# Attention operands in four buffers, loaded three pairs ahead, and the scatter DMAs of a pair issued one to each key block

## The chip, the cores and the metric

The kernel runs on 1 core of a Trainium2 chip. The metric is the time of one execution on the device in microseconds. The kernel before took 2875.18 us (median of 3 runs, 2851.36 to 2876.99).

## What is computed

A transformer layer on x of shape (8, 1024, 256), all in float32: x + attention(layernorm(x)) + mixture(layernorm(x)).

```
xn = layernorm(x)
# attention: 16 heads of 16 columns, bias alibi[h, q, k] = slope[h] * (k - q)
Q, K, V = xn @ Wq + bq, xn @ Wk + bk, xn @ Wv + bv
attn = softmax(Q K^T * 0.25 + alibi);  a = (attn V) @ Wo + bo
# mixture: each of the 8192 tokens goes to the 2 best of 8 experts, plus a shared expert
w = softmax(top2(xn @ Wg))
y = sum_e w[e] * (silu(xn W1[e]) * (xn W2[e])) W3[e]  +  (silu(xn Ws1) * (xn Ws2)) Ws3
out = x + a + y
```

## The kernel before

The work runs in four parts, one after the other. **Projections**: the 8192 tokens in 16 groups of 512; normalised rows go to `Xn` in DRAM, Q and K as a high and a low part to `QKh` and `QKl`, V to `Vd`. **Attention**: 64 pairs, a pair being two heads of one batch (8 batches of 8 pairs). **Experts**: 71 blocks of 256 token slots. **Shared expert and output**: 16 groups of 512 tokens.

One class, `Order`, writes down the order of all steps (`run`, L78, and `attention`, L206). Each engine runs through the same order in a subclass of its own (`Tensor`, `Scalar`, `Vector`, `Pool`, `Sync`) and issues its own share, so each engine's instructions, and each DMA queue's, stand in a fixed order. Engines wait for each other by counting semaphores; a wait blocks everything behind it on that engine.

A pair r has eight key blocks kc; a step s is 8r + kc, and `attention` works on even steps for two blocks at once. In the order `ORDER` (L42) TensorE alternates score matmuls ("S", 54 rows by 512 columns, into banks 0 to 3), maximum matmuls ("u", `max_unit`, 52 rows by 512, into a ring of banks 5 to 7) and, after four of each, the value matmuls of an earlier block ("P", `values`). ScalarE takes the exponential of the scores (L771). VectorE reduces each maximum matmul to row maxima (L916). The maxima must be known before a pair's scores are made; so the 32 maximum matmuls of a pair run ahead (`AHEAD`, 48 units, is one pair and a half): those of pair r+2 begin at step 8r + 4, those of pair r+1 end at step 8r + 2. Then VectorE makes 16 numbers of them (L920), GpSimd negates and splits them (L1178 to L1183), TensorE transposes them in the second half of step 8r + 4 (`max_rows`), ScalarE copies them (L760), and SP writes them into rows 52 and 53 of the pair's Q operand (L1354).

The operands of a pair are Q and K as stacked rows (high part, low part, high part, two rows of ones or of maxima, two of the bias) of 1024 columns, in the tile `OPS`, buffer r % 3. SP loads them in `load_pair` (L1328): 16 DMAs, 12 of 64 KB (L1344) and 4 of 8 KB from `Alid` (L1348, the last). `next_pair(r)` (L242) calls it at kc = 0 for pair r+2; between its second and third call stands `heads(r-1, 0)`, for which SP waits for pair r-1's sums (L778). Pairs 0 and 1 are loaded during the projections, pair 2 just before the loop. The rows of ones come from two memsets by GpSimd during the projections (L1135).

`heads` also normalises a finished pair: SP moves its sums out and back as a broadcast (`asum`, L1373, at kc = 4), GpSimd multiplies (L1190, at kc = 6), SP stores the result (L1377).

Beside attention runs the routing of tokens to experts: VectorE has one small operation every fourth step, GpSimd clears the 71 blocks of slots `Xs` and copies the expert weights together (pairs 0 to 9), and in pairs 34 to 49 (`SCAT_AT` = 34) GpSimd writes the normalised rows into their slots: per pair, after kc = 3, one load of 512 rows (L1218) and eight indirect DMAs of 128 rows (L1224), four row blocks by two chosen experts. Buffers `xr` alternate.

Of the kernel before, what the change touches and what calls it, by code (L numbers as in the profile page):

```python
# [7 lines left out]
F32 = mybir.dt.float32  # L8
# [6 lines left out]
P = 128  # L15
NB, S, D = 8, 1024, 256
# [5 lines left out]
NG = N // GT  # L22
# [5 lines left out]
NPAIR = NB * NH // 2  # L28
# [16 lines left out]
SCAT_AT = 34  # L45

SEMS = (

    "c_ident c_bor c_w1 c_w c_ali c_r x0 x1 x2 x3 xn0 xn1 xn2 qh0 qh1 ql0 ql1 vs0 vs1 op0 op1 op2 mx0 mx1 "
    "vst asd sdw asb ox0 ox1 zero wd xg0 xg1 sc0 sc1 wb0 wb1 wb2 xs0 xs1 xs2 xs3 yr0 yr1 xr0 xr1 oro ga0 ga1 ga2 ga3 res "  # L50

    "xt qkmm vmm mxmm mrt smm pv rtmm sct gmm up down sdn "
# [21 lines left out]
class Order:  # L74
# [3 lines left out]
    def run(self):  # L78
# [15 lines left out]
        n = 0  # L94
# [36 lines left out]
        while n < AHEAD:  # L131
            self.max_unit(n)
            n += 1
        for i in range(4):
            self.load_pair(2, i)
        for s in range(8 * NPAIR - 8):
            n = self.attention(s, n)
        for b in range(3):
# [2 lines left out]
        for s in range(8 * NPAIR - 8, 8 * NPAIR):  # L141
            n = self.attention(s, n)
# [3 lines left out]
        for s in range(8 * NPAIR, 8 * NPAIR + 2):  # L146
            n = self.attention(s, n)
# [58 lines left out]
    def attention(self, s, n):  # L206

        r, kc = divmod(s, 8)
        if s % 2 == 0:
            i = v = 0  # L210
            for c in ORDER:
                if c == "S":
                    if r < NPAIR:
                        self.scores(r, kc + i // 4, i % 2, i // 2 % 2)
                    i += 1
                elif c == "u":
                    if n < 32 * NPAIR:
                        self.max_unit(n)
                        n += 1
                else:  # L220
                    if v == 1 and kc == 4 and r + 1 < NPAIR:
                        self.max_rows(r + 1)
                    if s >= 2:
                        self.values(*divmod(s - 2 + v, 8))
                    v += 1
            if kc == 0:
                self.next_pair(r)
            elif r >= 1:
                self.heads(r - 1, kc // 2)
        if r < NE + 2 and kc == 1:  # L230
            self.pack_expert(r)
        if s < NBLK:
            self.clear_slots(s)
        if kc == 3 and SCAT_AT <= r < SCAT_AT + NG:
            self.scatter_group(r - SCAT_AT)
        if kc == 5 and r % 8 in (2, 3) and r < NPAIR - 8:
            self.load_v(r // 8 + 1, r % 8 - 2)
        if s % 4 == 3:
            self.route(s // 4)
        return n  # L240

    def next_pair(self, r):  # L242
        for i in range(4):
            if i == 2 and r >= 1:
                self.heads(r - 1, 0)
            if 1 <= r and r + 2 < NPAIR:
                self.load_pair(r + 2, i)


    def begin(self): pass  # L250
# [17 lines left out]
    def heads(self, r, i): pass  # L268
    def pack_expert(self, e): pass
    def clear_slots(self, s): pass  # L270
    def scatter_group(self, g): pass
    def route(self, i): pass
    def gather_weights(self, b): pass
    def load_slots(self, b): pass
# [42 lines left out]
def build(nc, t, out):  # L317
    ctx = ExitStack()
    with ctx:
        sem = {n: ctx.enter_context(nc.semaphore("s_" + n)) for n in SEMS}  # L320
# [15 lines left out]
        Xs = dram("Xs", [NSLOT, D])  # L336
# [6 lines left out]
        xn_v = Xn.rearrange("(g j p) d -> g p j d", p=P, j=4)  # L343
# [12 lines left out]
        slot = sbuf(ctx, "slot", [P, 2, NT], I32)  # L356
# [5 lines left out]
        mT = sbuf(ctx, "mT", [32, 2, P], F32R)  # L362
        xr = sbuf(ctx, "xr", [P, 2, 4, D])
        OPS = sbuf(ctx, "OPS", [P, 12 * S], F32R)
        QO = OPS[:, 0:3 * S].rearrange("p (k n) -> p k n", k=3)
        KO = OPS[:, 3 * S:6 * S].rearrange("p (k n) -> p k n", k=3)
        VB = sbuf(ctx, "VB", [P, 8 * S])
        vb = VB[:, :].rearrange("p (b c n) -> p b c n", b=2, c=8)

# [99 lines left out]
        class Tensor(Order):  # L469
# [71 lines left out]
            def max_unit(self, n, bank=None):  # L541
                r, u = divmod(n, 32)
                hh, i, half = 1 - u % 2, u // 4, u // 2 % 2
                k, h0 = r % 3, 64 * hh
                self.w.wait_ge(f"op{k}", 256 * (r // 3 + 1))
                if bank is None:
                    bank = self.ring_bank("max", n)
                else:
                    self.w.wait_ge("mxred", n)
                    if n >= 32:  # L550
                        self.w.wait_ge("mrev", 1)
                self.mm(ps[:, bank, :], QO[h0:h0 + KMAX, k, i * P:(i + 1) * P],
                        KO[h0:h0 + KMAX, k, half * GT:(half + 1) * GT], True, True).then_inc(sem["mxmm"], 1)

# [9 lines left out]
                          mneg[:, r % 2, :, :, :].rearrange("p h l i -> p (h l i)")).then_inc(sem["mrt"], 1)  # L564

            def scores(self, r, kc, hh, half):
                k, h0, n = r % 3, 64 * hh, 16 * r + 2 * kc + half
                bank = 2 * (n % 2) + hh
                self.w.wait_ge(f"op{k}", 256 * (r // 3 + 1))
                self.w.wait_ge(f"mx{r % 2}", 32 * (r // 2 + 1))  # L570
                if n < 2:
                    self.w.wait_ge("xh", NG)
                    self.w.wait_ge("xl", NG)
                self.w.wait_ge("exp", n - 1)
                if kc == 6 and half == 0:
                    self.w.wait_ge("mrev", min(r + 2, NPAIR))
                q = self.mm(ps[:, bank, :], KO[h0:h0 + KEXP, k, kc * P:(kc + 1) * P],
                            QO[h0:h0 + KEXP, k, half * GT:(half + 1) * GT], True, True)
                if hh == 1:
                    q.then_inc(sem["smm"], 1)  # L580
# [531 lines left out]
        class Pool(Order):  # L1112
# [15 lines left out]
            def pad(self, i):  # L1128
                e = self.e
                if i < 4:  # L1130
                    self.w.wait_ge("rstd", i + 2)
                    self.w.wait_ge("vad", i - 1)
                    self.w.wait_ge("pad", i)
                if i < 2:
                    e.memset(OPS[64 * i + 32:64 * i + 64, 0:6 * S].bitcast(F32), 1.0).then_inc(sem["pad"], 1)  # L1135
                elif i == 2:
                    e.memset(VB[:, :], 0.0).then_inc(sem["pad"], 1)
                elif i == 3:
                    e.memset(vb.rearrange("p b c (h d) -> p (b c) h d", d=32)[:, :, :, HD:HD + 1], 1.0
                             ).then_inc(sem["pad"], 1)  # L1140
# [71 lines left out]
                                 zero[:, :].rearrange("p (u d) -> p u d", u=1).broadcast_to([P, 2, D])  # L1212
                                 ).then_inc(sem["zero"], 16)

            def scatter_group(self, g):
                e, k = self.e, g % 2
                self.w.wait_ge(f"sc{k}", 128 * (g // 2))
                e.dma_start(xr[:, k, :, :], xn_v[g]).then_inc(sem[f"xg{k}"], 16)  # L1218
                self.w.wait_ge("rts", 2)
                self.w.wait_ge("zero", 16 * NBLK)  # L1220
                self.w.wait_ge(f"xg{k}", 16 * (g // 2 + 1))
                for i in range(4):
                    for c in range(2):
                        e.indirect_dma_start(  # L1224
                            Xs[:, :], bass.IndirectOffsetOnAxis(ap=slot[:, c, 4 * g + i:4 * g + i + 1], axis=0),
                            xr[:, k, i, :], None).then_inc(sem[f"sc{k}"], 16)

            def gather_weights(self, b):
                k = b % 3
# [52 lines left out]
        class Sync(Order):  # L1282
# [44 lines left out]

            def load_pair(self, r, i):  # L1328
                b, j = divmod(r, NH // 2)
                k = r % 3  # L1330
                at = slice(b * S, (b + 1) * S)
                done = sem[f"op{k}"]
                self.w.wait_ge("pad", 2)
                self.w.wait_ge("c_ali", 16)
                self.w.wait_ge("smm", 16 * (r - 2))
                self.w.wait_ge("mxmm", 32 * (r - 2))
                for f in range(2):
                    self.w.wait_ge(f"qh{f}", 16 * (b + 1))
                    self.w.wait_ge(f"ql{f}", 16 * (b + 1))
                dst, o, parts, al = ((QO, 0, (QKh, QKl, QKh), 1), (KO, D, (QKh, QKh, QKl), 0))[i // 2]  # L1340
                for n in (0, 1) if i % 2 == 0 else (2,):
                    for h in range(2):
                        h0 = o + 32 * j + HD * h
                        self.e.dma_start(dst[64 * h + 16 * n:64 * h + 16 * n + 16, k, :].bitcast(F32),  # L1344
                                         parts[n][h0:h0 + HD, at]).then_inc(done, 16)
                if i % 2:
                    for h in range(2):
                        self.e.dma_start(dst[64 * h + 48 + 2 * al:64 * h + 50 + 2 * al, k, :].bitcast(F32),  # L1348
                                         Alid[al, 2 * j + h, :, :]).then_inc(done, 16)

            def max_rows(self, r, bank=None):
                self.w.wait_ge("mrev", r + 1)
                for hh in range(2):
                    self.e.dma_start(QO[64 * hh + 52:64 * hh + 54, r % 3, :].bitcast(F32).rearrange("l (i n) -> l i n", n=P),  # L1354
                                     mT[16 * hh:16 * hh + 16, r % 2, :].bitcast(F32)).then_inc(sem[f"mx{r % 2}"], 16)

            def heads(self, r, i):
# [118 lines left out]
```

## Time and profile before

| | |
|---|---|
| median of 3 runs | 2875.18 us |
| the profiled execution, its own time | 2872.02 us |
| its span | 2870.2 us |
| mean granted TensorE clock | 0.943 |
| TensorE busy | 2639.1 us (92%) |
| VectorE busy | 2119.3 us (74%) |
| ScalarE busy | 1644.3 us (57%) |
| GpSimd busy | 854.4 us (30%) |
| chain that ended last: TensorE matmuls (L474) | 57% |
| the same: VectorE maxima (L916) | 8% |
| the same: SP issuing operand loads (L1344) | 6% |
| the same: landing of the last operand load (`OPS<-Alid`) | 3% |

Busy time is the sum over one engine's instructions. In the rows further down PE is TensorE, PEld its weight loads, DVE VectorE, ACT ScalarE, POOL GpSimd and SPq the DMA-issuing queue of SP. The granted clock is a share of full speed; it has two levels, 1.2 and 2.4 GHz, so that 0.5 is the low one. `OPS<-Alid` names a DMA by what it writes and reads. The chain is followed back from the last instruction through whatever released each step.

### The profile page before, as it was taken

How to read it: one execution, taken by the hardware profiler on the slowest of the kernel's cores; microseconds unless marked ns; L12 is line 12 of the kernel's file. 1: busy time of each engine (PE TensorE's matmuls, PEld its weight loads, DVE VectorE, ACT ScalarE, POOL GpSimd, SP SyncE). 2: the span in 40 equal slices, each digit the busy share in tenths (PEclk: the TensorE clock that was granted, in tenths of full speed). 3: DMA queues.
4: the chain of work that ended last, by engine and by line, in shares of the span. 5: the costliest groups of instructions: out<-in, count | busy, mean ns of one | idle time of the engine just before them, and what ended most of it. 6: DMA issues, size and time to landing. Idle time of an engine off the chain costs nothing.

```text
span 2870.2 us, 42979 instructions
## 1 busy us (share of the span) xinstructions
PE 2639.1 (92%) x16090; PEld 1624.0 (57%) x16090; DVE 2119.3 (74%) x3518; ACT 1644.3 (57%) x2314; POOL 854.4 (30%) x920
## 2 busy tenths in 40 slices
PE   5999889999999998888888999999999999999998
PEld 4774333333333333333333333399999998788887
DVE  7878777888988876766777888567777775545544
ACT  2445555666677665555655667767777773322322
POOL 4334433101101003434332100133343434434433
PEclk8998888999999987877888999999999999999999
DMA  5985553222222213333333211267777773433432
GB/s 194 349 297 181 175 176 123 73 59 69 70 62 76 61 53 104 107 100 111 106 102 95 66 58 58 97 213 233 244 237 242 241 232 88 122 89 95 120 95 74
DMA packets 213359, 383.62 MB, mean 134 GB/s; under 512 B 45264, under 2 KB 134544, under 8 KB 203792
## 3 DMA queue, kind: packets, MB, share of 16 engines
q1 hardware_dynamic: 175040, 218.25, 24.3%
q0 software_dynamic: 37024, 161.83, 17.8%
q8 instruction: 128, 2.10, 0.3%
q10 hardware_dynamic: 1088, 0.79, 0.1%
q14 instruction: 79, 0.65, 0.1%
HBM read 248.84 MB, written 141.43 MB: 136 GB/s over the span
## 4 chain that ended last, share of the span: by engine, by line
PE 59%; DVE 15%; SPq 8%; issue 6%; DMA 5%; ACT 5%; another core or an unknown queue 1%; POOL 1%; ACTq 0%; DVEq 0%; POOLq 0%
PE ps L474 57%; DVE mx L916 8%; SPq L1344 6%; DMA OPS<-Alid 3%; DVE OPS L1087 3%; PE ps L487 2%; ACT pta L771 2%; DVE VB L1084 2%; SPq L1365 1%; ACT OPS L843 1%; ACT accs L778 1%; DMA asum<-Sd 1%; SPq L1348 1%; DVE OL L1073 1%
## 5 line engine op out<-in xcount | busy, mean ns | idle before, releaser
L916 DVE TENSOR_REDUCE mx<-ps 128x1 f32<-128x512 f32 x2048 | 1277.0, 684 | 318.6 <-PE ps L474 277.5
L474 PE MATMUL ps<-OPS 52*128 52x512 f32 (+1 forms) x4096 | 964.7, 470 | 137.3 <-DMA OPS<-Alid 48.5
L474 PEld LDWEIGHTS ps<-OPS 52*128 52x128 f32 (+1 forms) x4096 | 501.7, 202 | 902.0 <-DVE mx L916 280.1
L771 ACT ACTIVATE pta<-ps 128x1024 f32<-128x1024 f32 x512 | 497.7, 1022 | 361.0 <-PE ps L474 329.0
L771 ACT ACTIVATE ptb<-ps 128x1024 f32<-128x1024 f32 x512 | 497.0, 1023 | 217.0 <-PE ps L474 207.6
L474 PE MATMUL ps<-OPS,WB 128*128 128x256 f32 (+1 forms) x2268 | 363.6, 312 | 4.2 <-DVE VB L1055 2.8
L474 PEld LDWEIGHTS ps<-OPS,WB 128*128 128x128 f32 x2268 | 310.5, 180 | 33.6 <-issue 4.8
L474 PE MATMUL ps<-ptb,VB 128*32 128x512 f32 x2048 | 310.3, 682 | 0.0
L474 PE MATMUL ps<-pta,VB 128*32 128x512 f32 x2048 | 287.9, 636 | 0.0
L474 PE MATMUL ps<-OPS,WB0c 128*128 128x256 f32 (+3 forms) x1440 | 257.9, 330 | 4.0 <-DVE WB0c L1038 3.0
L474 PEld LDWEIGHTS ps<-OPS,WB0c 128*128 128x128 f32 (+1 forms) x1440 | 210.3, 181 | 34.3 <-issue 5.1
L1190 POOL TENSOR_TENSOR accs<-accs,asum 128x512 f32<-128x512 f32 x64 | 82.4, 1288 | 488.8 <-DMA asum<-Sd 488.6
L474 PE MATMUL ps<-WB,OPS 128*128 128x256 f32 (+1 forms) x1422 | 189.7, 284 | 27.1 <-DVE OPS L1087 27.1
L1178 POOL TENSOR_SCALAR m<-m 128x16 f32<-128x16 f32 x64 | 19.5, 305 | 608.8 <-DVE m L920 608.8
L474 PEld LDWEIGHTS ps<-WB,OPS 128*128 128x128 f32 (+1 forms) x1422 | 178.7, 191 | 33.7 <-issue 33.6
L1060 DVE TENSOR_TENSOR OPS<-VB,OPS 128x256 fp32r<-128x256 f32 (+1 forms) x213 | 151.4, 711 | 37.2 <-ACT OPS L813 37.2
L837 ACT ACTIVATE VB<-ps 128x512 f32<-128x512 f32 (+1 forms) x96 | 57.1, 594 | 196.9 <-PE ps L474 196.9
L1087 DVE TENSOR_TENSOR OPS<-VB,OPS 128x512 fp32r<-128x512 f32 (+1 forms) x96 | 111.8, 1165 | 66.1 <-ACT OPS L843 39.3
L1224 POOL DMA_INDIRECT Xs<-xr,slot x128 | 124.7, 974 | 96.4 <-DMA xr<-Xn 62.2
L1098 DVE SCALAR_TENSOR_TENSOR VB<-gath,prob,ps 128x256 f32<-128x256 f32 x64 | 26.5, 477 | 162.3 <-PE ps L474 162.3
L843 ACT CAST OPS<-VB 128x512 fp32r<-128x512 f32 (+1 forms) x96 | 59.8, 623 | 145.4 <-DVE VB L1084 119.4
L1266 POOL DMA_INDIRECT gath<-Ys,slot x128 | 128.3, 1002 | 36.5 <-issue 35.2
(154 smaller groups left out, 2871.6 us busy)
## 6 DMA issues: line engine op xcount, KB each, us to landing
OPS<-QKh SPq DMA_DIRECT2D x512, 64.0 KB
Xs<-zero POOLq DMA_DIRECT2D x71, 256.0 KB, 3.6
xr<-Xs SPq DMA_DIRECT2D x71, 256.0 KB
Ys<-VB SPq DMA_DIRECT2D x71, 256.0 KB
QKh<-qkH SPq DMA_DIRECT2D x16, 1024.0 KB, 6.1
QKl<-qkL SPq DMA_DIRECT2D x16, 1024.0 KB, 8.4
OPS<-QKl SPq DMA_DIRECT2D x256, 64.0 KB
asum<-Sd SPq DMA_DIRECT2D x64, 256.0 KB
```

Source lines behind the costliest of these rows:

```text
L474: return self.e.matmul(o, l, r, start=start, stop=stop)
L487: return self.e.transpose(o, in_, ident[:, :])
L771: self.e.activation(pt(n), ps[:, b:b + 2, :], ACT.Exp).then_inc(sem["exp"], 1)
L843: self.e.copy(HH[0:hn, s, :], hf[0:hn, k, :]).then_inc(sem["hh"], 1)
L916: e.reduce_max(mx[:, k2, hh, i, half:half + 1], ps[:, bank, :], AX.X).then_inc(sem["mxred"], 1)
L1060: e.tensor_tensor(HL[0:hn, s, 0:BT], hfq[0:hn, k, :], HH[0:hn, s, 0:BT].bitcast(F32), ALU.subtract).then_inc(sem["hl"], 1)
L1084: e.tensor_tensor(hf[0:hn, k, :], ps[0:hn, 3 + 2 * (n % 2), :], sg[0:hn, k, :], ALU.mult).then_inc(sem["hf"], 1)
L1087: e.tensor_tensor(HL[0:hn, s, :], hf[0:hn, k, :], HH[0:hn, s, :].bitcast(F32), ALU.subtract).then_inc(sem["hl"], 1)
L1190: self.e.tensor_tensor(accs[:, r % 2, :], accs[:, r % 2, :], asum[:, :], ALU.mult).then_inc(sem["nrm"], 1)
L1224: e.indirect_dma_start(Xs[:, :], bass.IndirectOffsetOnAxis(ap=slot[:, c, 4 * g + i:4 * g + i + 1], axis=0), xr[:, k, i, :], None).then_inc ...
L1266: self.e.indirect_dma_start(gath[:, j, c, :], None, Ys[:, :], bass.IndirectOffsetOnAxis(ap=slot[:, c, i:i + 1], axis=0)).then_inc(sem[f"ga ...
L1344: self.e.dma_start(dst[64 * h + 16 * n:64 * h + 16 * n + 16, k, :].bitcast(F32), parts[n][h0:h0 + HD, at]).then_inc(done, 16)
```

## The change

The operands get four buffers in place of three: `QO` and `KO` take 4096 columns each of `OPS`, which had that room (12288 columns in all), the memsets cover 8192 columns, every `r % 3` becomes `r % 4`, and there is a semaphore `op3`. `load_pair` waits for the scores and maxima of three pairs back, is called three pairs ahead in `next_pair`, and pair 3 is loaded with pair 2 before the loop.

`scatter_group`, called once at kc = 3 of a pair, becomes `scatter_rows`, called at every kc. The first call of a pair also loads the rows; each call issues one of the eight indirect DMAs, after a wait for the scores of all blocks before its own (`smm` at least 16r + 2kc).

```diff
@@ Order.run
-        for i in range(4):
-            self.load_pair(2, i)
+        for r in (2, 3):
+            for i in range(4):
+                self.load_pair(r, i)
@@ Order.attention
-        if kc == 3 and SCAT_AT <= r < SCAT_AT + NG:
-            self.scatter_group(r - SCAT_AT)
+        if SCAT_AT <= r < SCAT_AT + NG:
+            self.scatter_rows(r - SCAT_AT, kc, 16 * r + 2 * kc)
@@ Order.next_pair
-            if 1 <= r and r + 2 < NPAIR:
-                self.load_pair(r + 2, i)
+            if 1 <= r and r + 3 < NPAIR:
+                self.load_pair(r + 3, i)
@@ build
-        QO = OPS[:, 0:3 * S].rearrange("p (k n) -> p k n", k=3)
-        KO = OPS[:, 3 * S:6 * S].rearrange("p (k n) -> p k n", k=3)
+        QO = OPS[:, 0:4 * S].rearrange("p (k n) -> p k n", k=4)
+        KO = OPS[:, 4 * S:8 * S].rearrange("p (k n) -> p k n", k=4)
@@ Tensor.max_unit and Tensor.scores
-                self.w.wait_ge(f"op{k}", 256 * (r // 3 + 1))
+                self.w.wait_ge(f"op{k}", 256 * (r // 4 + 1))
@@ Pool.pad
-                    e.memset(OPS[64 * i + 32:64 * i + 64, 0:6 * S].bitcast(F32), 1.0).then_inc(sem["pad"], 1)
+                    e.memset(OPS[64 * i + 32:64 * i + 64, 0:8 * S].bitcast(F32), 1.0).then_inc(sem["pad"], 1)
@@ Pool
-            def scatter_group(self, g):
+            def scatter_rows(self, g, i, n):
+
                 e, k = self.e, g % 2
-                self.w.wait_ge(f"sc{k}", 128 * (g // 2))
-                e.dma_start(xr[:, k, :, :], xn_v[g]).then_inc(sem[f"xg{k}"], 16)
+                if i == 0:
+                    self.w.wait_ge(f"sc{k}", 128 * (g // 2))
+                    e.dma_start(xr[:, k, :, :], xn_v[g]).then_inc(sem[f"xg{k}"], 16)
                 self.w.wait_ge("rts", 2)
                 self.w.wait_ge("zero", 16 * NBLK)
                 self.w.wait_ge(f"xg{k}", 16 * (g // 2 + 1))
-                for i in range(4):
-                    for c in range(2):
-                        e.indirect_dma_start(
-                            Xs[:, :], bass.IndirectOffsetOnAxis(ap=slot[:, c, 4 * g + i:4 * g + i + 1], axis=0),
-                            xr[:, k, i, :], None).then_inc(sem[f"sc{k}"], 16)
+                self.w.wait_ge("smm", n)
+                j, c = divmod(i, 2)
+                e.indirect_dma_start(
+                    Xs[:, :], bass.IndirectOffsetOnAxis(ap=slot[:, c, 4 * g + j:4 * g + j + 1], axis=0),
+                    xr[:, k, j, :], None).then_inc(sem[f"sc{k}"], 16)
@@ Sync.load_pair
-                k = r % 3
+                k = r % 4
...
-                self.w.wait_ge("smm", 16 * (r - 2))
-                self.w.wait_ge("mxmm", 32 * (r - 2))
+                self.w.wait_ge("smm", 16 * (r - 3))
+                self.w.wait_ge("mxmm", 32 * (r - 3))
```

## Rows read from the trace of the kernel before

**Rows 1.** Busy time by stretch of attention; columns end with clock, DMA share, GB/s.
```profile
259.00:580.00 321.00, 289.38 (x1558) 114.46 (x1556) 256.49 (x437) 195.13 (x218) 101.80 (x157) 0.88 0.43 136
580.00:1077.00 497.00, 465.89 (x2713) 182.54 (x2714) 431.18 (x738) 340.93 (x379) 50.03 (x92) 0.98 0.22 63
1077.00:1574.00 497.00, 433.04 (x2199) 169.61 (x2196) 346.39 (x579) 277.91 (x307) 180.75 (x222) 0.82 0.34 104
1574.00:1827.00 253.00, 238.45 (x1417) 93.20 (x1413) 221.81 (x374) 177.72 (x198) 23.36 (x46) 1.00 0.21 62
```

**Rows 2.** Timeline (start us, us): the copies ending pairs 0, 12, 33, 50, 61.
```profile
259.24 0.59 ACT L778 COPY accs<-ps 128x512 f32<-128x512 f32 x1
...
580.03 0.59 ACT L778 COPY accs<-ps 128x512 f32<-128x512 f32 x1
...
1076.83 0.59 ACT L778 COPY accs<-ps 128x512 f32<-128x512 f32 x1
...
1573.52 0.59 ACT L778 COPY accs<-ps 128x512 f32<-128x512 f32 x1
...
1827.40 0.59 ACT L778 COPY accs<-ps 128x512 f32<-128x512 f32 x1
```

**Rows 3.** Waits (us in total, times, longest) in the four stretches, in order.
```profile
PE ps L474 <- DMA OPS<-Alid: 18.2, 11, 3.6
...
PE ps L474 <- DMA OPS<-Alid: 10.0, 21, 1.5
...
PE ps L474 <- DMA OPS<-Alid: 15.7, 9, 6.0
...
PE ps L474 <- DMA OPS<-Alid: 4.5, 11, 0.6
```

**Rows 4.** Timeline of a calm pair's middle, around the last operand load.
```profile
1666.12 2.48 DVE L916 TENSOR_REDUCE mx<-ps 128x1 f32<-128x512 f32 x4 [0.22 <-PE ps L474]
...
1668.84 2.48 DVE L916 TENSOR_REDUCE mx<-ps 128x1 f32<-128x512 f32 x4 [0.23 <-PE ps L474]
...
1669.86 0.57 SPq L1348 DMA_DIRECT2D OPS<-Alid  x2
...
1672.07 1.77 PE L474 MATMUL ps<-OPS 52*128 52x512 f32 x7 [0.57 <-DMA OPS<-Alid]
...
1672.60 2.49 DVE L916 TENSOR_REDUCE mx<-ps 128x1 f32<-128x512 f32 x4 [0.90 <-PE ps L474]
```

**Rows 5.** Timeline of VectorE after a long load wait in the first stretch.
```profile
404.93 2.48 DVE L916 TENSOR_REDUCE mx<-ps 128x1 f32<-128x512 f32 x4 [2.25 <-PE ps L474]
409.10 2.48 DVE L916 TENSOR_REDUCE mx<-ps 128x1 f32<-128x512 f32 x4 [1.69 <-PE ps L474]
```

**Rows 6.** Timeline of one burst of scatters: first, eighth, and VectorE beside it.
```profile
1417.71 1.03 POOL L1224 DMA_INDIRECT Xs<-xr,slot  x1 [3.85 <-DMA xr<-Xn]
...
1421.86 2.49 DVE L916 TENSOR_REDUCE mx<-ps 128x1 f32<-128x512 f32 x4 [0.23 <-issue]
...
1426.65 0.96 POOL L1224 DMA_INDIRECT Xs<-xr,slot  x1 [0.30 <-issue]
...
1427.67 1.29 DVE L916 TENSOR_REDUCE mx<-ps 128x1 f32<-128x512 f32 x2 [3.33 <-remote]
```

**Rows 7.** Waits in the third stretch with no releaser on record.
```profile
DVE mx L916 <- remote: 25.4, 9, 4.3
```

**Rows 8.** GpSimd: a normalisation and a negation (timeline); the row load's landing.
```profile
1660.80 1.28 POOL L1190 TENSOR_TENSOR accs<-accs,asum 128x512 f32<-128x512 f32 x1 [11.25 <-DMA asum<-Sd]
...
1671.63 0.25 POOL L1178 TENSOR_SCALAR m<-m 128x16 f32<-128x16 f32 x1 [9.55 <-DVE m L920]
...
DMA to landing us min/median/max: 4.2/4.4/5.3
```

**Rows 9.** Timeline: the second memset and the VectorE operation beside it.
```profile
28.15 5.70 DVE L890 TENSOR_SCALAR xn<-xt,mv,rstd 128x256 f32<-128x256 f32 x2 [0.54 <-POOL rstd L1126]
28.17 5.21 POOL L1135 MEMSET OPS<- 32x6144 f32 x1
```

More of the change, by code:

```diff
@@ L47 @@
 SEMS = (
-    "c_ident c_bor c_w1 c_w c_ali c_r x0 x1 x2 x3 xn0 xn1 xn2 qh0 qh1 ql0 ql1 vs0 vs1 op0 op1 op2 mx0 mx1 "
+    "c_ident c_bor c_w1 c_w c_ali c_r x0 x1 x2 x3 xn0 xn1 xn2 qh0 qh1 ql0 ql1 vs0 vs1 op0 op1 op2 op3 mx0 mx1 "
     "vst asd sdw asb ox0 ox1 zero wd xg0 xg1 sc0 sc1 wb0 wb1 wb2 xs0 xs1 xs2 xs3 yr0 yr1 xr0 xr1 oro ga0 ga1 ga2 ga3 res "
@@ L270, in clear_slots, with scatter_rows @@
     def clear_slots(self, s): pass
-    def scatter_group(self, g): pass
+    def scatter_rows(self, g, i, n): pass
     def route(self, i): pass
@@ L543, in max_unit @@
                 hh, i, half = 1 - u % 2, u // 4, u // 2 % 2
-                k, h0 = r % 3, 64 * hh
-                self.w.wait_ge(f"op{k}", 256 * (r // 3 + 1))
+                k, h0 = r % 4, 64 * hh
+                self.w.wait_ge(f"op{k}", 256 * (r // 4 + 1))
                 if bank is None:
@@ L566, in scores @@
             def scores(self, r, kc, hh, half):
-                k, h0, n = r % 3, 64 * hh, 16 * r + 2 * kc + half
+                k, h0, n = r % 4, 64 * hh, 16 * r + 2 * kc + half
                 bank = 2 * (n % 2) + hh
-                self.w.wait_ge(f"op{k}", 256 * (r // 3 + 1))
+                self.w.wait_ge(f"op{k}", 256 * (r // 4 + 1))
                 self.w.wait_ge(f"mx{r % 2}", 32 * (r // 2 + 1))
@@ L1353, in max_rows @@
                 for hh in range(2):
-                    self.e.dma_start(QO[64 * hh + 52:64 * hh + 54, r % 3, :].bitcast(F32).rearrange("l (i n) -> l i n", n=P),
+                    self.e.dma_start(QO[64 * hh + 52:64 * hh + 54, r % 4, :].bitcast(F32).rearrange("l (i n) -> l i n", n=P),
                                      mT[16 * hh:16 * hh + 16, r % 2, :].bitcast(F32)).then_inc(sem[f"mx{r % 2}"], 16)
```

## The prediction

> **What bounds the kernel now.** I read the views in this order: the stages, the pair boundaries, the waits on the operand loads, one calm pair at close range, then the same pair where the clock is low and where the scatters run.
>
> The stage table [rows 1] shows TensorE busy for 90% and more of every attention stage, but at a granted clock of 0.88, 0.98, 0.82 and 1.00. The evictions at pair ends [rows 2] cut the same stretches into pairs: 12 pairs in 320.8 us (26.7 each), 21 in 496.8 (23.7), 17 in 496.7 (29.2), 11 in 253.9 (23.1). One pair is the same work throughout, so the late stage is the kernel undisturbed, and the first and third stages carry an excess: 3.6 us by 12 pairs and 6.1 us by 17.
>
> TensorE waits for the last operand load (the Alid rows) once in nearly every pair: 18.2, 10.0, 15.7 and 4.5 us by stage [rows 3]. In a calm pair [rows 4] four maxima start at 1666.12 and at 1668.84, a step of 2.72 us, and the next four at 1672.60, a step of 3.76: the Alid load was issued at 1669.86 and TensorE got it at 1672.07, 0.57 us late.
>
> A longer wait costs more than itself. After one that left VectorE idle for 2.25 us the steps go from 404.93 to 409.10 [rows 5], which is 4.17 us for the work of 2.72. A microsecond at the low clock (1.2 of 2.4 GHz) thus wastes 1 - 2.72/4.17 = 0.35 us. By the mean clock, 2 x (1 - 0.88) = 24% of the first stage, 77 us, and 2 x (1 - 0.82) = 36% of the third, 179 us, ran low [rows 1].
>
> The third stage is the one with the scatters. A burst of eight runs from 1417.71 to 1427.61 [rows 6]; VectorE ends its maxima at 1424.35 and gets the next only at 1427.67, when the last scatter has been issued. The records name no releaser; nine such holds sum to 25.4 us on VectorE [rows 7]. The first five scatters of that burst go by without a hold.
>
> **The change, part by part.** *Loads three pairs ahead.* The same sixteen DMAs of a pair are issued by SP at the same place and behind the same counts of finished score and maximum matmuls, since both the buffer count and the distance grow by one. They are needed a whole pair, some 23 us, later than now; the largest wait to be hidden is 6 us. Every such wait goes except that of pair 2, loaded just before the loop as now. Pair 3 is now loaded there too: sixteen more issues, about 8 us of SP (two Alid issues take 0.57 us [rows 4], the others are similar), while SP's next duty is half a pair away. In exchange the loop's last load falls away.
> What is late next in the calm boundary step is VectorE itself: it has two small operations there. The gain is between the wait alone, 4.5/11 = 0.4 us a pair, and the whole 1.04 us of the longer step; I take 0.6, nearer to the wait as VectorE is nearly full, so a pair is worth 22.5.
> - Late stage: 11 x 0.6 = 7 us.
> - Second stage: from 23.7 to 22.75 a pair (22.5 and a quarter for the routing operations that run there) gives 19 us; the bounds are its waits, 10, and 25 at 22.5.
> - First stage: from 26.7 to 23.2 (more routing, and a heavier DMA load) gives 42 us. From the other side: waits of 18.2 and 0.35 x 77 = 27 for the clock are 45.
>
> *Scatters spread.* The third stage at 22.6 a pair instead of 29.2 would give 112 us. From the other side: 0.35 x 179 = 62 for the clock, 15.7 for load waits, 25.4 or more of holds: 103 and up. Of this the loads own 15.7, their 0.6 a pair where no wait shows, and the low clock behind them; I put that at 33, and 79 to the bursts.
> They will not be one to each block. GpSimd's queue is in order, and three things stand in it: the normalisation, which starts at 1660.80 [rows 8], just ahead of a pair's end; the scatters of blocks 6 and 7 behind it, 2 x 1.27 us [rows 6]; then the load of the next rows, about 1 to issue, as for a scatter, and 4.4 to land, with GpSimd waiting for it [rows 8]. That is 1662.1 + 2.5 + 5.4 = 1670.0. Scatters 0 and 1 then end at 1672.5, the negation of the maxima, due at 1671.63, starts 0.9 us late, and scatters 2 to 5 follow at once, as the score blocks they wait for are done or nearly: a run of six with a gap of some 0.8, the negation's, then a run of two. Behind the negation TensorE's transpose is two steps (5.4 us) away, so its 0.9 us cost nothing; if that cover is gone, see the third rival. The waits on score counts release themselves and hold nothing that is due. Six in a run is near where the hold began (after 6.6 us), so I keep back 20 us. The term is 92; ends 33 and 112.
> On this the Trainium skill, SBUF — State Buffer, section "SBUF: two separate sides", speaks against the change: engine ports and DMA ports are disjoint and neither side can slow the other. By that rule the holds are none of the scatters' doing, and the term would be 33, not 92. The rows put the hold's end on the burst's end, so I go by them.
>
> *Padding for the fourth buffer.* Two memsets on GpSimd grow from 6144 to 8192 columns. One takes 5.21 us [rows 9], so 6.95, +1.74 each. A VectorE operation that starts with it lasts 5.70 us, to the memset's end, and TensorE waits out that stretch: nothing hides it, +3.5 us (from 0, were it not on the path).
> The Trainium skill, same page and section, calls the pair of ports shared by GpSimd and VectorE an exclusive lock; the 5.70 us agree.
>
> *Rest.* The new wait names no other engine's queue; buffers and later stages reuse the same memory after attention ends. Nothing changes from 1865 us on.
>
> **Sum.** 42 + 19 + 92 + 7 - 3.5 = 156 us off the profiled execution's own 2872.0: 2716 us. The median of the runs shown is 3 us above it, and they spread from 2851 to 2877.
>
> **The rivals.**
> 1. *The holds stay*, moved into the run of six. For: no row names what holds the engines; the run of six. Against: five scatters pass free, and the end of the hold is the end of the burst. Term 33 in place of 92: 2872 - (42 + 19 + 33 + 7 - 3.5) = 2775.
> 2. *Depth helps, another load-like wait follows it* (the maxima rows of the next pair, or the broadcast of the sums, late in the first stage's traffic). The first stage then gives half, and the clock stays low there: 2716 + 21 = 2737, inside the forecast's range.
> 3. *GpSimd's queue becomes the bound in the scatter pairs.* If the normalisation comes over 4.5 us later than in the calm pair (5.4 less 0.9), the transpose waits, and each of 16 pairs pays some 2 us and 8 us at the low clock, 5 in all: +80, 2796; with rival 1, 2855, which is no change.
> 4. *Slower: every scatter holds the engines by itself.* Place: each of the 16 scatter pairs, eight times. If one hold of about 0.8 us per block keeps the clock low, a pair costs 8 x (4.17 - 2.72) = 11.7 and 8 x 0.8 = 6.4 more than 22.5; 16 x 18.1 = 290 against the 112 of excess now, less the 64.5 of the other terms: +113, 2985. It decides from any hold that keeps the clock low throughout. Against it: the free first five.
>
> **How the numbers follow.** The forecast with rival 2 has 0.62, rival 1 0.23, rival 3 0.10 (half of it with rival 1), rival 4 0.05. The forecast's own range is 2680 (every term at its better end) to 2755. To hold 8 in 10 the range goes on through rival 1 and the milder rival 3: 2680 to 2800. A measurement of this kernel tells about 1%, 29 us. Faster by more has 0.88, within it 0.07 (rival 3 with 1, and part of what no case names), slower 0.05.
>
> **What would show each step.** Right: no wait on the Alid load after pair 2; clock near 1.0 in the first stage; pairs of 22.4 to 22.8 in the late stage; scatter pairs near 23 to 24 with no hold of over 1 us on VectorE; the memsets at 6.95. Scatters in runs of six and two would confirm the queue's reading. Wrong: holds at the end of each run of six (rival 1), TensorE's transpose waiting for GpSimd (3), a clock near 0.5 through the third stage (4), or boundary steps still above 3.3 us with the loads long landed.

## The result and the profile after

The changed kernel took 2719.6 us (median of 4 runs, 2717.9 to 2722.7) beside 2865.4 us of the kernel before (4 runs, 2851.4 to 2877.0): a ratio of 0.949, 95% interval 0.944 to 0.955. Its profiled execution has a span of 2717.9 us against 2870.2 and a mean granted clock of 0.982 against 0.943. Timed again in another placing (a placing is a chip and the time at which it was used), beside the kernel before there, it took 2720.8 us against 2835.5: 0.960 (0.955 to 0.964). The change is worth 4 to 5%. The changed kernel ran alike in both placings and the kernel before did not, which matters below. The three later placings were on three chips; the record doesn't name the chip of the first, so it is open whether the chip made the difference.

The copies that end pairs 0, 12, 33, 50 and 61 of the changed kernel, as in [rows 2] (timeline: start, duration):

```profile
262.88 0.59 ACT L779 COPY accs<-ps 128x512 f32<-128x512 f32 x1
...
560.50 0.59 ACT L779 COPY accs<-ps 128x512 f32<-128x512 f32 x1
...
1033.49 0.59 ACT L779 COPY accs<-ps 128x512 f32<-128x512 f32 x1
...
1430.57 0.59 ACT L779 COPY accs<-ps 128x512 f32<-128x512 f32 x1
...
1674.58 0.59 ACT L779 COPY accs<-ps 128x512 f32<-128x512 f32 x1
```

The stages between them, in the view of [rows 1] (busy time of TensorE, its weight loads, VectorE, ScalarE and GpSimd, then clock, DMA share, GB/s):

```profile
263.00:561.00 298.00, 269.41 (x1558) 106.20 (x1557) 254.57 (x438) 195.20 (x218) 101.33 (x157) 0.95 0.46 147
561.00:1033.00 472.00, 445.81 (x2707) 174.70 (x2703) 428.27 (x737) 339.62 (x378) 49.93 (x93) 1.00 0.24 66
1033.00:1431.00 398.00, 370.63 (x2203) 145.87 (x2200) 342.40 (x581) 276.40 (x308) 181.23 (x221) 0.97 0.44 130
1431.00:1675.00 244.00, 233.96 (x1423) 91.88 (x1420) 220.59 (x375) 178.31 (x199) 23.28 (x46) 1.00 0.21 60
```

VectorE is busy with the same reductions for as long as before, but in shorter stretches, and the clock is 0.95 to 1.00 where it was 0.82 to 1.00. By the copies the stages went from 320.8, 496.8, 496.7 and 253.9 us to 297.6, 473.0, 397.1 and 244.0. That is 23.2 + 23.8 + 99.6 + 9.9 = 156.5 us; the first pair ends 3.6 us later, and what lies behind pair 61 takes 0.5 more: 152.3, the difference of the spans.

The boundary step of a calm pair, as in [rows 4]:

```profile
1500.16 2.48 DVE L917 TENSOR_REDUCE mx<-ps 128x1 f32<-128x512 f32 x4 [0.22 <-PE ps L475]
1502.68 0.19 DVE L921 TENSOR_REDUCE m<-mx 128x16 f32<-128x32 f32 x1
1502.78 0.24 DVE L926 RECIPROCAL sq<-sq 128x16 f32<-128x16 f32 x1
1502.94 2.42 DVE L917 TENSOR_REDUCE mx<-ps 128x1 f32<-128x512 f32 x4
1505.59 2.48 DVE L917 TENSOR_REDUCE mx<-ps 128x1 f32<-128x512 f32 x4 [0.24 <-PE ps L475]
```

The step from 1500.16 to 1502.94 takes 2.78 us instead of 3.76, and the next 2.65: TensorE no longer waits for a load there, and VectorE's two small operations are absorbed. A calm pair takes 22.18 us against 23.08.

A pair that is still long, in the scatter stage of the changed kernel (pair 35, 25.4 us; the lines show its first half):

```profile
1058.85 0.59 SPq L1368 DMA_DIRECT2D sq<-accs  x1
...
1063.35 0.25 DVE L926 RECIPROCAL sq<-sq 128x16 f32<-128x16 f32 x1 [1.91 <-DMA sq<-accs]
...
1063.99 0.99 POOL L1227 DMA_INDIRECT Xs<-xr,slot  x1 [5.69 <-DMA xr<-Xn]
1064.20 0.50 PE L475 MATMUL ps<-OPS 52*128 52x512 f32 x1 [2.08 <-DVE mx L917]
...
1065.29 0.97 POOL L1227 DMA_INDIRECT Xs<-xr,slot  x1 [0.30 <-issue]
1066.30 0.29 POOL L1179 TENSOR_SCALAR m<-m 128x16 f32<-128x16 f32 x1
...
1067.43 1.06 POOL L1227 DMA_INDIRECT Xs<-xr,slot  x1 [0.20 <-issue]
```

Two things are to be seen. VectorE, whose instructions are in order, stands at the reciprocal of the finished pair's sums until SP's fetch of those sums (`sq<-accs`) lands, 4.5 us after its issue; TensorE then waits for VectorE, 2.1 us. This is the wait that took the load's place. The issue itself is late as well: SP issued the fetch 3.2 us after the start of the copy that ends the pair (1055.67), where 0.6 us is the usual figure. And GpSimd issues scatters 0 and 1 when the row load has landed, then the negation of the maxima, then scatters 2 to 5: the order that the prediction worked out. With scatters 6 and 7 behind the normalisation, they go out in runs of two, two and four.

The memsets (source line; min/median/max in ns, then first and last start) and the VectorE operation beside the second, as in [rows 9]:

```profile
L1136 POOL MEMSET OPS<- x2: 6919/6920/6921, 19.2 to 29.7; 32x8192 f32 x2
```
```profile
29.67 7.41 DVE L891 TENSOR_SCALAR xn<-xt,mv,rstd 128x256 f32<-128x256 f32 x2 [0.54 <-POOL rstd L1127]
```

### The profile page after: what moved, and what is told of

Same layout as the page of the kernel before. It is cut to its first block, busy times and chain, and to the rows that moved or that the text cites. A ratio compares the mean times of both kernels' runs of the same rounds, so it can differ in the third digit from the quotient of the medians.

```text
span 2717.9 us, 42994 instructions
## 1 busy us (share of the span) xinstructions
PE 2527.5 (93%) x16090; PEld 1580.8 (58%) x16090; DVE 2114.4 (78%) x3518; ACT 1639.8 (60%) x2314; POOL 858.1 (32%) x920
## 4 chain that ended last, share of the span: by engine, by line
PE 62%; DVE 22%; issue 6%; ACT 5%; DMA 4%; SPq 1%; POOL 1%; ACTq 0%; DVEq 0%; POOLq 0%
PE ps L475 60%; DVE mx L917 13%; DVE OPS L1088 3%; ACT pta L772 2%; PE ps L488 2%; DVE VB L1085 2%; DMA sq<-accs 2%; ACT OPS L844 1%; SPq L1347 1%; DVE OL L1074 1%; ACT OPS L826 1%; DMA WR0c<-Wd,widx 1%; DVE VB L1105 0%; DVE xn L891 0%; DMA xt<-in_x 0%
## 5 line engine op out<-in xcount | busy, mean ns | idle before, releaser
L917 DVE TENSOR_REDUCE mx<-ps 128x1 f32<-128x512 f32 x2048 | 1270.6, 681 | 160.2 <-PE ps L475 152.3
L475 PE MATMUL ps<-OPS 54*128 54x512 f32 (+1 forms) x4096 | 897.0, 443 | 89.3 <-DVE mx L917 41.3
L475 PEld LDWEIGHTS ps<-OPS 52*128 52x128 f32 (+1 forms) x4096 | 461.6, 189 | 797.2 <-DVE mx L917 279.3
L475 PE MATMUL ps<-ptb,VB 128*32 128x512 f32 x2048 | 279.7, 619 | 0.0
L475 PE MATMUL ps<-pta,VB 128*32 128x512 f32 x2048 | 276.2, 612 | 0.0
L1061 DVE TENSOR_TENSOR OPS<-VB,OPS 128x256 fp32r<-128x256 f32 (+1 forms) x213 | 152.3, 715 | 35.8 <-ACT OPS L814 35.8
```

Source lines behind the costliest of these rows:

```text
L475: return self.e.matmul(o, l, r, start=start, stop=stop)
L917: e.reduce_max(mx[:, k2, hh, i, half:half + 1], ps[:, bank, :], AX.X).then_inc(sem["mxred"], 1)
L1061: e.tensor_tensor(HL[0:hn, s, 0:BT], hfq[0:hn, k, :], HH[0:hn, s, 0:BT].bitcast(F32), ALU.subtract).then_inc(sem["hl"], 1)
```

## The experiments

The theory at the start was the prediction's: load waits and scatter bursts each cost by themselves (A). The rival (B): what shows at a burst comes from meeting the loads. All stage times are differences of the copies' starts in one profiled execution each; the two kernels without holds, before again and memsets only, differ by 12 us in the third stage, so a few microseconds there mean little. The kernel before took 2836.1 us beside the spread-only, four-buffers, memset and plain-DMA kernels, 2835.5 beside the second runs and both sums-first kernels, and 2838.1 beside the last two.

| kernel | median us | ratio to before, 95% | stage 1 | stage 2 | stage 3 | stage 4 |
|---|---|---|---|---|---|---|
| before, first profile | 2865.4 | | 320.8 | 496.8 | 496.7 | 253.9 |
| before again | 2835.2 (one run) | | 319.0 | 500.1 | 458.9 | 253.8 |
| memsets only | 2839.3 (one run) | | 314.4 | 494.1 | 470.7 | 255.3 |
| spread only | 2817.7 | 0.992 (0.990-0.995) | 318.4 | 490.3 | 446.7 | 253.8 |
| four buffers only | 2738.3 | 0.964 (0.960-0.968) | 294.8 | 473.1 | 422.2 | 244.1 |
| changed, first profile | 2719.6 | 0.949 (0.944-0.955) | 297.6 | 473.0 | 397.1 | 244.0 |
| changed again | 2720.8 | 0.960 (0.955-0.964) | 296.4 | 473.0 | 401.7 | 244.1 |
| four buffers, plain DMAs in a burst | 2709.1 (one run) | | 297.6 | 473.1 | 387.0 | 244.0 |
| sums first, burst | 2702.2 | 0.952 (0.949-0.956) | 283.0 | 472.8 | 392.5 | 244.1 |
| sums first | 2695.3 | 0.950 (0.946-0.954) | 281.9 | 473.0 | 386.0 | 244.0 |
| rows ahead | 2687.0 | 0.945 (0.942-0.949) | 288.2 | 473.0 | 377.2 | 244.1 |
| late pad | 2689.0 | 0.945 (0.942-0.949) | 287.6 | 473.1 | 377.3 | 244.1 |

**Four buffers only.** The changed kernel with its burst back:

```diff
-        if SCAT_AT <= r < SCAT_AT + NG:
-            self.scatter_rows(r - SCAT_AT, kc, 16 * r + 2 * kc)
+        if kc == 3 and SCAT_AT <= r < SCAT_AT + NG:
+            for i in range(8):
+                self.scatter_rows(r - SCAT_AT, i, 0)
```

> The changed kernel with the eight scatters again in one burst after kc = 3 (four buffers and three pairs ahead stay). Theory A (the holds belong to the burst, whatever the loads do): stages 1, 2 and 4 as in the changed kernel (297.6, 473.0, 244.0 us), the 17 pairs of the third stage keep holds of 2 to 4 us at the burst's end and a low clock behind them, 397 + about 79 = 460 to 480 us; total about 2795 us, 0.975 of before. Rival B (the holds came from the burst meeting operand loads that were wanted at once): third stage 390 to 410 us, total about 2725 us.

It is neither. The third stage is 422.2 us, below A's 460 and above B's 410, and no wait without a releaser is on record in it. VectorE's waits in that stage (us, times, longest) are for the fetch of the sums:

```profile
DVE sq L927 <- DMA sq<-accs: 23.6, 12, 8.8
```

Why the fetch is late here stands in the timeline of one such pair, from the burst's last scatter on:

```profile
1110.92 0.96 POOL L1228 DMA_INDIRECT Xs<-xr,slot  x1 [0.30 <-issue]
1111.90 1.29 POOL L1192 TENSOR_TENSOR accs<-accs,asum 128x512 f32<-128x512 f32 x1
1112.84 0.59 ACT L780 COPY accs<-ps 128x512 f32<-128x512 f32 x1
1113.22 0.34 SPq L1381 DMA_DIRECT2D OTd<-accs  x1
1113.79 0.79 SPq L1348 DMA_DIRECT2D OPS<-QKh  x2
...
1117.99 0.60 SPq L1369 DMA_DIRECT2D sq<-accs  x1
...
1119.91 0.25 DVE L927 RECIPROCAL sq<-sq 128x16 f32<-128x16 f32 x1 [1.31 <-DMA sq<-accs]
```

GpSimd's normalisation of the pair before stands behind the burst; SP's queue stands at the store of the normalised rows (`OTd<-accs`) until it is done, and the eight loads and then the fetch come behind that store. From issue to reciprocal the fetch takes only 1.9 us. Eleven of the twelve waits are of this kind: 1.9 to 2.6 us from issue to reciprocal, but an issue 4.3 to 6.1 us after the copy's start. The twelfth is issued 10.0 us after it. With four buffers a burst costs through this chain, from GpSimd's queue to SP's to VectorE's, and not by holding the engines.

**Spread only.** The kernel before with `scatter_rows` and its call in place of `scatter_group`.

> The kernel before (three buffers, two pairs ahead) with the scatters spread as in the changed kernel. Theory A: no hold without releaser in the third stage, but load waits stay; stages 1, 2 and 4 as before (320.8, 496.8, 253.9 us), third stage 497 - 79 = about 418 to 435 us; total about 2790 to 2805 us, 0.975 of before. Rival B: third stage still 480 us and more, total within 1% of before. If the two parts add, the gains of this run and of the four-buffers-only run sum to 152 us; if one needs the other they sum to less.

The gain is 0.8% (0.5 to 1.0), not 2.5%. With that of four buffers alone it sums to the whole: 98 + 18 = 116 us, where the changed kernel gained 115 when it was timed again. So the parts add, within what the runs can tell, and theory A's sizes are wrong. TensorE's load waits in the third stage remain, all of them:

```profile
PE ps L474 <- DMA OPS<-Alid: 26.8, 17, 2.7
```

**Memsets only.**

```diff
-  e.memset(OPS[64 * i + 32:64 * i + 64, 0:6 * S].bitcast(F32), 1.0)
+  e.memset(OPS[64 * i + 32:64 * i + 64, 0:8 * S].bitcast(F32), 1.0)
```

> The kernel before with the two memsets widened from 6144 to 8192 columns and nothing else. Memsets of 6.95 us each; the first pair's sums are copied at about 262.8 us in place of 259.24 (both memsets on the path, +3.5); if only one were on it, about 261.0; if none, 259.2. Nothing else moves.

The memsets take 6.92 us. The first copy is at 263.4 us, 4.2 later than in the first profile and 1.9 later than in the second profile of the kernel before (261.5). That starting time varies from execution to execution by more than one memset's share, so this run alone leaves the size between 1.9 and 4.2. All profiles together say more: the three with both early memsets short have the copy at 259.2, 261.5 and 259.7 us, the eight with them wide at 262.9 to 265.6, with means of 260.1 and 263.8. That is 3.6 us, near the forecast 3.5, though seven of the eight differ in more than the memsets. The surprise was elsewhere: the same bursts, and none of the holds of [rows 6, 7].

**Before again.** The kernel before, unchanged.

> The kernel before, word for word, profiled beside the next kernels. If the holds without a releaser in the third stage belong to the kernel, they are there again, 25 us and more, in ten bursts or more, and the third stage takes about 497 us. If they belonged to the one execution or chip that was profiled first (the memset run, with the same bursts, had none and took 471 us there), none is there and the third stage takes 465 to 475 us.

No hold. Its third stage takes 458.9 us, and its waits there are for loads, more of them than in [rows 3]:

```profile
PE ps L474 <- DMA OPS<-Alid: 42.4, 17, 9.4
DVE sq L925 <- DMA sq<-accs: 15.2, 2, 7.8
```

So the holds do not come with the code alone. They were there in the first profile, in a placing where the kernel before took 2851 to 2877 us, and absent in all ten profiles of the three later placings; four of these have the same scatter bursts. A hold of TensorE would also give a late load time to land, which would explain why 15.7 us of load waits were seen with holds and 42.4 without (53.3 in memsets only); no run shows this by itself.

**Plain DMAs in a burst.** Four buffers only, with each scatter replaced by a plain DMA of the same 128 KB to fixed rows, so that the rows do not reach their experts' slots and the kernel's result is wrong:

```diff
-  e.indirect_dma_start(Xs[:, :], bass.IndirectOffsetOnAxis(ap=slot[...], axis=0), xr[:, k, j, :], None)
+  e.dma_start(Xs[(8 * g + i) * P:(8 * g + i + 1) * P, :], xr[:, k, j, :])
```

> As the four-buffers-only kernel, but each of the eight indirect DMAs of the burst is a plain DMA of the same 128 KB from the same rows to fixed, contiguous rows of the slots (so the rows do not reach their experts' slots), still issued by GpSimd. If the holds come from the generation of descriptors for scattered rows by GpSimd: no hold, third stage near 380 to 400 us. If they come from eight 128 KB writes in a row from GpSimd's queue, whatever the form: holds as with the scatters, third stage 460 us and more.

387.0 us, 35 below the burst of scatters, and no hold. As the burst of scatters had no hold beside it either, this can't tell what made them. What it does show: the sums' fetch is waited for 4.9 us in this stage, against 23.6 with the scatters. GpSimd is through with eight plain DMAs in 4.3 us and with eight scatters in 9.9 (1101.94 to 1111.88), so the normalisation, and SP's queue behind it, are held up less:

```profile
1097.60 4.30 POOL L1228 DMA_DIRECT2D Xs<-xr  x8 [3.67 <-DMA xr<-Xn]
```

**Changed again.** The changed kernel, unchanged.

> The changed kernel, word for word, timed beside the kernel before on one chip: the size of the change where the kernel before ran at 2836 us. If the first comparison's two sides were equally placed: ratio 0.949, about 2692 us there. If the kernel before alone varies from chip to chip and the changed one does not: about 2719 us, ratio 0.959.

0.960 and 2720.8 us: the kernel before is what varied. Between the two profiles of this placing the stages gain 22.6 + 27.1 + 57.2 + 9.8 us, 116.0 with the start and the tail.

**Sums first.** One reordering in the changed kernel:

```diff
     def next_pair(self, r):
+        if r >= 1:
+            self.heads(r - 1, 0)
         for i in range(4):
-            if i == 2 and r >= 1:
-                self.heads(r - 1, 0)
             if 1 <= r and r + 3 < NPAIR:
                 self.load_pair(r + 3, i)
```

> The changed kernel with one reordering in next_pair: SP fetches the finished pair's sums before all four operand loads, not between the second and the third. Theory: what is late next in the first and third stages is VectorE's reciprocal, which waits for that fetch (13 waits, 43.9 us with one of 25 at the end of attention), standing in the DMA queues behind the loads of Q. With the fetch ahead of 8 of the 64 KB loads it lands earlier: the pairs of 25 to 30 us go down to 22.2 to 24, first stage 285 us, third stage 380 to 385 us, total about 2690 us. Rival (the fetch is slow because of the software queue's traffic, not of the loads): same waits, 2719 us.

2695.3 us, 25 less than the changed kernel beside it (runs of 2691.9 to 2699.2 against 2717.6 to 2728.0). Besides the wait at the end of attention, the fetch is waited for once, 1.1 us. The first stage gets 14.4 us shorter and the third 15.6 (in these two profiles the part behind pair 61 is 7.5 longer, so the spans differ by 21.9). The rival falls, but the edit does two things, and each has its stage. In the first stage of the changed kernel's second profile SP issued the waited fetches 0.6 to 2.0 us after the copy, and they landed 5.5 to 7.4 us after that: what held them was on the way, the loads issued just before. In the third stage it issued them up to 5.2 us after the copy, behind its store and eight loads. With the fetch first, SP issues it 0.6 us after the copy in every pair of both stages. What is left in the third stage are two pairs, 26.4 and 26.0 us; the first:

```profile
1073.13 0.99 POOL L1227 DMA_INDIRECT Xs<-xr,slot  x1 [6.73 <-DMA xr<-Xn]
1074.43 0.97 POOL L1227 DMA_INDIRECT Xs<-xr,slot  x1 [0.31 <-issue]
1075.44 0.29 POOL L1179 TENSOR_SCALAR m<-m 128x16 f32<-128x16 f32 x1
...
1076.72 0.28 PE L488 MATMUL ps<-ident,mneg 128*32 128x128 f32 x1 [3.29 <-POOL mneg L1184]
```

The row load took over 6.7 us, two scatters and the negation stood behind it, and TensorE's transpose waited 3.3 us. That is the third rival of the prediction, in 2 pairs of 16. The other wait is 1.6 us.

**Sums first, burst.** The same with the burst edit shown above.

> As the sums-first kernel, but with the eight scatters in one burst after kc = 3 again. If the spread helped only by shortening the wait of the reciprocal, this is within 10 us of the sums-first kernel (third stage 380 to 395 us). If a burst costs by itself even with four buffers, the third stage stays near the 422 us of the four-buffers-only kernel, 25 us above the changed kernel.

Within 10 us, as the first theory had it: 392.5 against 386.0 in the third stage, 2702.2 against 2695.3 in all. The runs don't overlap (2700.8 to 2703.8 against 2691.9 to 2699.2), so the burst still costs some 7 us. They are in two pairs (29.5 and 30.3 us). There GpSimd's normalisation stands behind the burst and also behind a load of V, for which GpSimd waits, and ends 8.9 and 7.0 us after the copy; SP issues the fetch 9.4 and 7.4 us after it, and it lands 2.0 us later:

```profile
DVE sq L927 <- DMA sq<-accs: 9.2, 2, 5.5
```

**Rows ahead.** Sums first, with the row load moved:

```diff
+        if kc == 4 and SCAT_AT <= r + 1 < SCAT_AT + NG:
+            self.scatter_load(r + 1 - SCAT_AT)
...
-                if i == 0:
-                    self.w.wait_ge(f"sc{k}", 128 * (g // 2))
-                    e.dma_start(xr[:, k, :, :], xn_v[g]).then_inc(sem[f"xg{k}"], 16)
+            def scatter_load(self, g):
+                k = g % 2
+                self.w.wait_ge(f"sc{k}", 128 * (g // 2))
+                self.e.dma_start(xr[:, k, :, :], xn_v[g]).then_inc(sem[f"xg{k}"], 16)
```

> The sums-first kernel with the load of a scatter group's 512 rows issued half a pair earlier (at kc = 4 of the pair before), so that GpSimd no longer waits for it at kc = 0 with the negation of the maxima queued behind. Theory: in the sums-first kernel the two long scatter pairs (26.4 and 26.0 us) are TensorE's transpose waiting 3.3 and 1.6 us for the negation (the third rival of the prediction), because the row load took 6.7 us; they go to 22.2 to 22.6, the third stage from 386 to 378 us, the total from 2695 to about 2688 us. The scatters then go out one to a block. Rival (the negation is late because of the operand and V loads, not of the row load): no change in the third stage.

All 17 pairs of the third stage take 22.2 us, 377.2 in all, the granted clock is 1.00, and the total is 2687.0 us. The first stage takes 288.2 us in this profile (287.6 in the next kernel's), against 281.9 with the sums first alone; why is not shown. That a scatter goes out one to a block is not so: the normalisation still comes at the pair's end, and four scatters follow it (GpSimd's timeline):

```profile
1110.97 1.28 POOL L1194 TENSOR_TENSOR accs<-accs,asum 128x512 f32<-128x512 f32 x1 [5.57 <-DMA asum<-Sd]
1112.39 1.00 POOL L1227 DMA_INDIRECT Xs<-xr,slot  x1
1113.70 0.97 POOL L1227 DMA_INDIRECT Xs<-xr,slot  x1 [0.31 <-issue]
1114.97 0.96 POOL L1227 DMA_INDIRECT Xs<-xr,slot  x1 [0.30 <-issue]
1116.24 0.96 POOL L1227 DMA_INDIRECT Xs<-xr,slot  x1 [0.30 <-PE ps L478]
1120.77 0.26 POOL L1182 TENSOR_SCALAR m<-m 128x16 f32<-128x16 f32 x1 [3.57 <-DVE m L924]
```

The runs of four cost nothing at all: the scatter pairs are as short as the calm ones. The negation now finds GpSimd idle.

**Late pad.** Rows ahead, with the early memsets at 6144 columns and two of 2048 three groups later (`pad` steps 4 and 5).

> The rows-ahead kernel with the memset of the fourth buffer's share taken out of the two early memsets (6144 columns again) and done as two memsets of 2048 columns three groups later. Theory: the first pair's sums are copied at 259.5 to 260.5 us instead of 263.5, since VectorE has slack in the later groups; total 3 to 3.5 us less, about 2684 us. Rival (a memset costs wherever it stands, because VectorE waits it out): still 263 us.

The first copy is at 262.95 us against 264.95, the late memsets take 1.80 us each, and the total is the same within the runs (2680.7 to 2692.6 against 2682.4 to 2688.5). Two microseconds of the expected 3.5 at most, and not told apart from no change. Inconclusive.

## Why the prediction was right, point by point

The total, 2716 us against 2719.6, is right, and the late stage (7 forecast, 9.9 measured), the second (19, 23.8) and the memsets (6.95 us each, 6.92) are near. The agreement to 4 us is largely luck. The first stage gave 19 us less than forecast, and the other three 15 more (99.6 against 92 in the third, 4.8 and 2.9 in the second and the last). And the gain of 156 was counted from a profile that held 25.4 us of waits without a releaser on VectorE alone, which no later one has: timed again, the same change gave 115 us. Of the signs named for being right, the clock of the first stage (0.95, not near 1.0) and the calm pairs (22.18 us, not 22.4 to 22.8) missed. TensorE was also not busy for 90% of every stage before: in the third it is 433.0 of 497 us, 87%.

- **Loads three pairs ahead.** Right: TensorE waits 0.5 us for an Alid load in the whole changed kernel, against 48.5. The gain of a calm pair was mis-sized: 0.6 was taken near the wait alone, and 0.9 was measured, near the other end, 1.04; VectorE's two small operations cost the steps beside them next to nothing (2.78 and 2.65 us, mean 2.72).
- **First stage, 42 us, measured 23.2.** Here the step "what is late next" failed. It named VectorE's own two operations, and missed that one of them, the reciprocal, waits for a DMA which SP issues behind half of the pair's loads. It cost 7.5 us of waits there in the changed kernel, with a clock of 0.95. With the fetch ahead of the loads the stage gives 39 us (320.8 to 281.9), at 1.00. The second rival had the size (half of the stage) and the kind, but neither of the two transfers that it named: it was the fetch of the sums, not their broadcast.
- **Third stage, 92 us, measured 99.6, for the wrong reason.** The step that failed is the split: 33 to the loads, 79 to bursts that hold the engines. Of the 99.6 us, 38 (496.7 to 458.9) are what the first profile of the kernel before has and its second has not, the holds among it (26 if memsets only, 470.7, is the measure); four buffers took 37 (458.9 to 422.2; 49 from 470.7), and the spread 20 to 25 (422.2 to 401.7 or 397.1). The spread does so by letting GpSimd reach the normalisation sooner, which lets SP issue the sums' fetch sooner: its wait falls from 23.6 us to 14.3 in one profile and 9.7 in the other:

```profile
DVE sq L926 <- DMA sq<-accs: 9.7, 6, 2.7
```

- **The rule weighed.** The Trainium skill, SBUF — State Buffer, section "SBUF: two separate sides", has engine and DMA ports disjoint, by which the holds were none of the scatters' doing. The prediction went by the rows, that a hold ended with the burst, and the later runs are against it: with the same scatter bursts four later profiles show none (before again, memsets only, four buffers only, sums first with the burst), nor does the one with plain DMAs. This agrees with the rule, but doesn't prove it, as the holds themselves stay unexplained. One profiled execution showed two things together, and that was taken for cause. By the rule the term was 33, by the rows 92; the stage gained 99.6 us in the first placing and 57.2 when both kernels were profiled again.
- **GpSimd's queue.** The order came as worked out, with the run of six split in two and four by the negation. Two sizes did not. From the row load's issue to the first scatter it took 5.7 to 6.9 us in the changed kernel, not 5.4, and the negation was up to 4.9 us late, not 0.9. And the cover behind it is not 5.4 us: in a calm pair of the changed kernel TensorE's transpose starts 3.2 us after the negation's last operation has ended. So the third rival needed less than the 4.5 us of further delay that it named. In the first profile of the changed kernel the transpose still never waits for GpSimd in the scatter stage, and in the second once, 0.8 us, as TensorE is itself late; with the sums first it waits in two pairs, 4.9 us together, and that is the last wait left.
- **Slower, if every scatter holds the engines.** Excluded: in the rows-ahead kernel eight scatters a pair cost 0.0 us a pair against a calm one.

What stays open: what the holds of the first profile were. In the one of [rows 6] VectorE and ScalarE stood for 3.3 us each and TensorE for 3.2, and holds were in no later execution that was profiled. As the changed kernel's profile of the first placing has no burst in it, it is also open whether the spread removed them there; a burst kernel run in that placing would tell.

## What to carry to other kernels

When a wait is taken away by loading earlier, look at every small transfer that shares the queues with the loads and at every engine that stands in order behind one: a fetch of 8 KB put ahead of the loads gave 25 us here, more than the spread of the scatters (18). When a DMA lands late, read its issue first: in the scatter stage here the issuing queue stood at a store that waited for another engine's work. A wait for which the profile names no releaser should be seen in a second execution before a term of the sum is built on it. And a stall of TensorE has to be priced with the microseconds at a low clock behind it, which here were up to four times the stall itself.

## What the runs showed of the hardware

- The kernel before differs by 1.1% between placings (median 2865.4 us in the first, 2836.1, 2835.5 and 2838.1 in the three others) where the changed kernel does not (2719.6 and 2720.8). Within the later placings the executions of the kernel before go from 2827.3 to 2852.5 us, at granted clocks from 0.959 to 0.947: the longer ones have the lower clock.
- An 8 KB fetch from SP landed 4.5 us after its issue in the long pair above, with 16 operand DMAs, two scatters and a row load issued around it, and 5.5 to 7.4 us after it where it was waited for in the first stage; issued late in the four-buffers kernel, it took 1.9. With eight loads moved behind it the waits fell from 23.0 us (48.1 less the 25.1 of the last pair) to 1.1.
- What a TensorE stall leaves behind it does not follow its length. In the kernel before (TensorE's timeline: start, duration, idle before), after a wait of 0.84 us for a load:

```profile
1029.42 2.07 PE L474 MATMUL ps<-OPS 52*128 52x512 f32 x7 [0.84 <-DMA OPS<-Alid]
1031.42 1.93 PE L474 MATMUL ps<-ptb,VB 128*32 128x512 f32 x8
1033.28 2.38 PE L474 MATMUL ps<-OPS 54*128 54x512 f32 x8
...
1040.20 1.06 PE L474 MATMUL ps<-pta,VB 128*32 128x512 f32 x8
```

The 39 product matmuls from 1029.42 to 1040.20 took 10.8 us with one transpose (0.4) among them, where 39/16 of 2.72 us are 6.6: 3.7 us more, four times the wait. The granted clock is 0.50 from 1030 to 1040, the low level, and 1.00 from 1041 on. In the changed kernel the wait of 2.08 us above was followed by 17 product matmuls and a transpose (0.27) in 4.8 us (1064.20 to 1068.98), where 17/16 of 2.72 are 2.9: 1.6 us more, less than the wait; the clock is 0.50 from 1065 to 1068 and 1.00 from 1069 on. What decides between the two is not shown here.
